# A completion count between the row scatters of GpSimd, one behind the other

## The reference

```python
# mixer: projection to 2 x 256, causal convolution of 4 taps, a gated linear recurrence, projection back
xz = x @ W_in.T;  x_proj, z = split(xz)
x_conv = silu(conv1d(x_proj, conv_w) + conv_b)
Bm, Cm, dt_in = split(x_conv @ W_x.T)
alpha = sigmoid(0.1 * softplus(dt_in @ W_dt.T + b_dt))
h = scan(clip(alpha, 0.01, 0.99), (1 - alpha) * sigmoid(mean(Bm)) * x_conv)
out = ((h * sigmoid(mean(Cm)) + D * x_conv) * silu(z)) @ W_out.T
# experts: 8 experts of width 256, the two best of each token, weights by softmax of their two logits
h = silu(xt @ w1[e]) * (xt @ w3[e]);  y = h @ w2[e]
out[t] = sum over the two chosen e of prob[t, e] * y[e, t]
```

## Time and profile before

| | |
|---|---|
| Runs | 473.81, 474.22, 474.67 us |
| Profiled execution | 472.82 us, its span 471.0 us |
| PE busy | 428.5 us (91%) |
| DVE busy | 394.9 us (84%) |
| ACT busy | 289.3 us (61%) |
| POOL busy | 311.1 us (66%) |
| Scatters into `moe_in`, line 593 | 128, mean 1034 ns |
| Scatters into `moe_out`, line 608 | 142, mean 1036 ns |

### The profile page before, as it was taken

How to read it: one execution, slowest core, us unless ns; L and a number is a source line. 1 busy time by engine, 2 the same in 40 slices (tenths; PEclk the granted TensorE clock), 3 DMA queues, 4 the chain that set the end, 5 groups by cost and what they waited for, 6 DMA issues and landing times.

```text
span 471.0 us, 8361 instructions
## 1 busy us (share of the span) xinstructions
PE 428.5 (91%) x2440; PEld 306.9 (65%) x2440; DVE 394.9 (84%) x836; ACT 289.3 (61%) x406; POOL 311.1 (66%) x344
## 2 busy tenths in 40 slices
PE   0889969999999999998999999999999999989771
PEld 0877524555545555554888889889888998644461
DVE  5999985999999999997998997767767775699981
ACT  2793476788898888899364444344444553878710
POOL 3657777777777777660377777777777777776300
PEclk9999999999999999999999999999999999999997
DMA  8951126122121313143667766566556662019996
GB/s 244 290 174 43 52 101 188 52 66 81 52 92 51 97 52 97 35 119 109 171 204 218 231 203 191 177 186 189 168 159 188 179 181 89 21 52 226 210 214 147
DMA packets 48078, 65.93 MB, mean 140 GB/s; under 512 B 8424, under 2 KB 30223, under 8 KB 48048
## 3 DMA queue, kind: packets, MB, share of 16 engines
q1 hardware_dynamic: 36240, 39.56, 30.1%
q0 software_dynamic: 10656, 24.47, 18.6%
q10 hardware_dynamic: 1152, 1.57, 1.1%
HBM read 42.09 MB, written 33.83 MB: 161 GB/s over the span
## 4 chain that ended last, share of the span: by engine, by line
PE 48%; DVE 33%; issue 11%; ACT 5%; DMA 1%; DVEq 0%; SPq 0%; ACTq 0%
PE PD L893 13%; DVE hbuf L1398 6%; PE PB L725 4%; DVE hbuf L1409 4%; PE PD L836 3%; PE PA L859 3%; PE PB L855 3%; PE PA L855 3%; PE PB L859 3%; PE PB L856 3%; PE PA L856 3%; DVE gbuf L1380 3%; DVE y L1418 2%; DVE gbuf L1283 2%; DVE xacc L1496 2%
## 5 line engine op out<-in xcount | busy, mean ns | idle before, releaser
L608 POOL DMA_INDIRECT moe_out<-xnT,dst_u x142 | 147.2, 1036 | 63.4 <-issue 33.7
L593 POOL DMA_INDIRECT moe_in<-xn,slot_u x128 | 132.3, 1034 | 44.6 <-issue 39.1
L1196 ACT ACTIVATE xn<-PA 128x1024 f32<-128x1024 f32 (+1 forms) x36 | 36.5, 1015 | 64.3 <-PE PA L859 54.9
L893 PE MATMUL PD<-xnT,xn 128*128 128x128 f32 x536 | 65.7, 275 | 0.0
L1623 DVE TENSOR_TENSOR xn<-xn,PB 128x1024 f32<-128x1024 f32 (+1 forms) x36 | 43.4, 1205 | 25.5 <-PE PB L859 20.5
L893 PEld LDWEIGHTS PD<-xnT,xn 128*128 128x128 f32 x536 | 62.8, 192 | 0.5 <-issue 0.5
L740 PE MATMUL PC<-xc,Wc 128*128 128x512 f32 x128 | 57.8, 594 | 2.9 <-ACT xc L1093 2.9
L753 PE MATMUL PA<-xnT,Wtap 128*128 (+4 forms) x128 | 58.2, 598 | 0.0
L753 PEld LDWEIGHTS PA<-xnT,Wtap 128*128 128x128 f32 x128 | 24.9, 194 | 31.6 <-issue 31.6
L740 PEld LDWEIGHTS PC<-xc,Wc 128*128 128x128 f32 x128 | 23.2, 190 | 26.8 <-issue 23.4
L1486 DVE SCALAR_TENSOR_TENSOR acc<-PA,cw,acc 128x510 f32<-128x510 f32 (+2 forms) x48 | 35.5, 740 | 1.8 <-ACT acc L1082 1.4
(11 more groups left out here) (244 smaller groups left out, 922.9 us busy)
## 6 DMA issues: line engine op xcount, KB each, us to landing
xnT<-moe_w SPq DMA_DIRECT2D x36, 256.0 KB
xn<-moe_in SPq DMA_DIRECT2D x31, 266.0 KB
out_dram<-moe_out POOLq DMA_DIRECT2D x12, 512.0 KB, 15.3
xnT<-moe_w SPq DMA_DIRECT2D x36, 128.0 KB, 2.1
out_dram<-xacc SPq DMA_DIRECT2D x7, 512.0 KB, 3.5
moe_out<-xnT,dst_u POOLq DMA_INDIRECT x142
moe_in<-zrow SPq DMA_DIRECT2D x8, 266.0 KB, 3.5
moe_w<-in_L_ffn_w_dram SPq DMA_DIRECT2D x2, 1024.0 KB
```

What stands on the lines that cost most here:

```text
L593: gp.indirect_dma_start(xs_dram, bass.IndirectOffsetOnAxis(ap=slot_u[:, k, j:j + 1], axis=0), xn_row[:, j, :], None).then_inc(s_scat, 16)
L608: gp.indirect_dma_start(yt_dram, bass.IndirectOffsetOnAxis(ap=dst_u[:, t, j:j + 1], axis=0), yo[t % OUTS][:, j, :], None, bounds_check=lim ...
L893: last = pe.matmul(PD[:, 512 + j * D:512 + (j + 1) * D], hid[b][:, k * SLOTS + j * P:k * SLOTS + (j + 1) * P], (w2x[t - FULL] if mixed and ...
L1196: act.activation(halves(sil, t), halves(PA[:, :], t), ACT.Silu).then_inc(s_sil, 1)
```

## The change

A new semaphore `s_desc` is counted up by one by each of the 270 scatters, on GpSimd itself (`engine_sem`), beside the 16 of the DMA that tell of the landing. Ahead of every scatter but the first stands a wait until the count of the one before it is there (`BEHIND` is 1). In both loops the new wait comes after the waits that were there.

```diff
+BEHIND = 1
...
+        s_desc = sem("s_desc")
...
                         follow(j * TOP_K + k)
+                        if j * TOP_K + k >= BEHIND:
+                            gp.wait_ge(s_desc, j * TOP_K + k + 1 - BEHIND)
                         gp.indirect_dma_start(xs_dram, bass.IndirectOffsetOnAxis(ap=slot_u[:, k, j:j + 1], axis=0),
-                                              xn_row[:, j, :], None).then_inc(s_scat, 16)
+                                              xn_row[:, j, :], None, engine_sem=s_desc).then_inc(s_scat, 16)
...
                         gp.wait_ge(s_T, min(t + 4, MOE_TILES))
+                    gp.wait_ge(s_desc, TOP_K * TILES + t * GT + j + 1 - BEHIND)
                     gp.indirect_dma_start(yt_dram, bass.IndirectOffsetOnAxis(ap=dst_u[:, t, j:j + 1], axis=0),
-                                          yo[t % OUTS][:, j, :], None, bounds_check=limit, oob_is_err=False).then_inc(s_ys[t % OUTS], 16)
+                                          yo[t % OUTS][:, j, :], None, bounds_check=limit, oob_is_err=False,
+                                          engine_sem=s_desc).then_inc(s_ys[t % OUTS], 16)
```

## The result

The changed kernel takes 596.29 us (median of four runs, 595.65 to 596.61) against 474.45 us (473.81 to 475.46): 1.2581 times as long, with a 95% interval of 1.2555 to 1.2607. The prediction was 590 us, range 508 to 612, slower at 0.93. Lines have moved: 593 to 597, 608 to 613, 622 to 628, 836 to 842, 1684 to 1690, 462 to 464.

The account below looks back on a forecast made before the run. POOL's last scatter was taken to set the end, one for one. Profiled 472.8 + 48.6 (first loop) + 1 (clock) + 67.7 (second loop) = 590.1; plus 1.4 for the median, less 1.5 for queues: 590 us, range 508 to 612.

Parts of the forecast that it names:

- Counting: Both loops: each scatter telling of its own end on GpSimd costs nothing, taken as 0.
- Scatters 1 to 20: First loop, where the new wait is the only one: 0.01 us each, 0.2 in all, bounds 0 and 0.07 each.
- 107 + 141 others: Both loops, another wait ahead of the scatter: exposed decoding makes the gap 0.78 us for 0.30, 0.48 more each.
- Last scatter of first loop: First loop's end: waits make it 51.6 us later, less 1.7 us for scatters running while DVE is still.
- Second loop: Experts' scatters on POOL: 141 waits at 0.48 us lengthen the loop by 67.7 us, to about 257 us.
- Last scatter's end to end of span: Tail: POOL's last scatter sets the end one for one, the span ending 50.0 us after it.
- the term of -1.7 us for fewer meetings with DVE: First loop: 24 scatters run while DVE is still and take 0.96 us in place of a mean of 1.034.
- Rival D: Scatters in both loops: holding POOL to one step removes pauses, 7.6 us, giving 468 us; chance 0.03.
- slack: SP's load between the loops: it has about 1.3 us to spare before PE's start, taken off the delay.
- the 1 us put down for the clock: Start of the experts' phase: after 47 us of idle PE, 1 us added for the 1.2 GHz clock level.
- the 1.5 us taken off for fewer stores on the queues: Sums in the tail: they may meet fewer stores on the queues, so 1.5 us comes off the total.
- the 1.4 put on for the runs over the profiled one: Whole kernel: the median of the runs is 1.4 us above the profiled execution, so that is added.

## Why the prediction was right

The mechanism (a stand-alone wait that ends with the scatter before exposes what comes ahead of the next) and the size of its price came as forecast. Step by step:

| Step | Predicted | Measured |
|---|---|---|
| Counting | 0 | 0 (473.61 against 473.62 us) |
| Scatters 1 to 20 | 0.01 each | gap 0.30 to 0.31 |
| 107 + 141 others | gap 0.78 | 0.78 first loop, 0.76 to 0.79 second |
| Last scatter of first loop | +49.9 us | +54.7 |
| First scatter of second loop | +49.6 | +53.55 |
| Second loop | +67.7 | +69.8 |
| Last scatter's end to end of span | 50.0 | 49.5 |
| Span | 588.3 | 593.9 |

**The end is GpSimd's.** 53.55 + 69.8 - 0.5 = 122.9 = 593.9 - 471.0. The page's chain of before named PE and DVE and "issue" for 11%; the kernel with waits in the second loop alone shows that it was the last scatter, and POOL's DRAIN is what stands last in the trace. The prediction had the sums landing at about 465 and POOL's program ending "only then"; the 5.6 us between the landing and 470.7 are that DRAIN, which it left out without harm, since it is as long in both kernels.

**Which wait is carried.** I read from two rows with two waits that an instruction carries its first wait and the others stand ahead. That is so: 107 instructions on line 596, and 475.82 us when the order is turned. For the carried wait the prediction calls the trace in agreement with 50 to 100 ns; that was generous, since 0.31 against 0.30 us is only 0.01. The Trainium skill says of instructions waiting on multiple engines that EventSemaphore instructions may be put ahead of them ("Perfetto Trace Analysis", Identifying Dependency Chains); it doesn't say what that costs, and here the order of writing alone makes 120 us. That the scatter's decoding is what is exposed was my reading. The runs bear out the place (what stands behind the unmet wait) and the split (0.08 us for a wait there, 0.47 us more than the usual gap for a scatter); what the sequencer does in the 0.47 us no row shows.

**The first loop was 4.8 us too short.** Gaps and start gave 51.0 us more (50.7 in idle time, 0.3 in the start), as the sum said (51.6). The miss is the term of -1.7 us for fewer meetings with DVE: the scatters got longer in sum, 136.0 for 132.3. The 28 that run while DVE is still do take 0.96 us. But the 100 others rose from a mean of 1.03 to 1.09: as many scatters are long (34 over 1.05 us, as before), but the longest 20 are longer. Beside DVE's scan (line 1398, now 1404) they take 1.61 us where it was 1.29. They begin 0.38 us into it and not 0.69, so both end 1.98 us after the scan began. The others take 1.44 or 1.45 beside another instruction (line 1415) than the 1.27 of before (line 1380). I had the number of meetings as what counts, and where in the DVE instruction the scatter begins counted as much.

**Second loop, 2.1 us too short.** 141 x 0.47 is 66.3 us. The bars give 1.6 us more, and pauses without a releaser the rest: 2.92 us ahead of the loop's 114th scatter (the first loop has its long pause ahead of the 114th too), 1.1 to 1.2 ahead of four others. With `BEHIND` at 2, or the new wait first, the first of them is 1.63 or 1.64, and before the change it isn't there. Rival D had expected the wait to remove pauses. That it shows some which a scatter had covered is my reading; no run shows what they are.

**The rest.** SP's load had 1.7 us of slack (+54.57 at the load, which was issued at 266.63, +52.86 at PE, which started at 216.62 before) for 1.3 predicted, and from PE's start to the first result it took 13.26 us for 12.56, 0.7 for the 1 us put down for the clock, which was at 0.50 there. The experts' last result came at 487.89, 56 us ahead of the last scatter's end (53 predicted).

The spans account for 5.6 of the 6.3 us between 590 and 596.3. The rest comes from two allowances: the 1.5 us taken off for fewer stores on the queues, where the tail was 0.5 shorter, and the 1.4 put on for the runs over the profiled one, which was 0.6.

## What to carry to other kernels

Where an engine issues long instructions back to back, the gap between two of them can be short (0.30 us here), by my reading because the next is taken in while one runs. A wait for the one before costs next to nothing if it is the wait that the instruction carries, and 0.47 us for an indirect DMA if it stands alone ahead of it; so write the wait that is met last first, or wait for the one before last. Count that price as often as the loop runs, and look at the end of the span for whose last instruction sets it: an engine that is busy for 66% of it can be the one.

## What the runs showed of the hardware

- In the programs as built, up to two waits share one stand-alone instruction, and the new wait's place among them is not always the one written. By the semaphores in the records, with one met wait added behind the new one they share one instruction (gap 0.75 to 0.77). With two added behind it, the new wait is in the last of two instructions (0.75 to 0.77), with one ahead and two behind in the first of two (0.83 to 0.86).
- A scatter's count on GpSimd comes with the end of its bar: a stand-alone wait for it is over at 64.2 where the bar ends at 64.21, and with the carried wait the next scatter starts 0.30 us after that end, as without any wait. The Trainium skill says that the profiler's end of such a DMA is the end of descriptor making and not of the data ("Perfetto Trace Analysis", DMA Instruction — SWDGE (GPSIMD)); the trace agrees, the rows of a scatter land a median of 2.9 us after its issue.
- Scatters of GpSimd are longer beside certain instructions of DVE, and how much depends on where in the DVE instruction they begin: one that begins 0.69, 0.43 or 0.38 us into the scan takes 1.29, 1.55 or 1.61 us (the kernel before, the one with two waits added ahead, the change), so that it ends 1.98 or 1.99 us after the scan began. Alone it takes 0.96.
